# Three layers of a six-layer decoder: channel mix as a pipeline of single batches, relative attention's start reordered, mLSTM's mask and line products in 16-bit parts

## The chip, the cores and the metric

The kernel runs on one core of a Trainium2 chip. Its time is the device time in microseconds from the start of the program to its end. A core has a matrix engine (PE; its weight loads are shown as PEld), a vector engine (DVE), an activation engine (ACT), a general engine (POOL) and a queue that issues most DMAs (SP). They run side by side and are ordered by semaphores that the kernel sets and waits for by hand.

## The reference, cut

x is (8, 256, 256): 8 batches, 256 tokens, 256 features. Two blocks of three layers, each followed by a sum with its input and a normalisation; what matters here are the third, fourth and fifth layers.

```
# third layer, channel mix
x_prev = x shifted by one token, zero first
xr = mu_r*x + (1-mu_r)*x_prev ;  xk = mu_k*x + (1-mu_k)*x_prev
out = sigmoid(xr @ W_r.T) * (square(relu(xk @ W_k.T)) @ W_v.T)

# fourth, attention of 16 heads with relative embeddings
scores = q.k + q.rel_k[clip(distance)] ;  out = (P @ v + P @ rel_v[...]) @ W_out

# fifth, mLSTM with 4 heads; q from x, k and v from the context
cs = cumsum(log_sigmoid(fg)) ;  log_D[s,t] = cs[s] - cs_before[t] + ig[t], -inf for t > s
D = exp(log_D - max_t log_D) ;  C = (q.k/8) * D
h = C @ v / (max(|sum C|, exp(-max log_D)) + eps), normalised per head
```

## The kernel before

`program` calls six layers one after another: retention, cross attention, channel mix, relative attention, mLSTM and a last expert layer. Each has a block of five instruction streams and writes its result to memory; the next layer's first DMA goes out after the previous one's last store has landed. All matmuls here are fp32 except one group in the last layer. A product of fp32 shows as two records in the trace, one of 16 bits and a transposition as one.

**Channel mix** (`channel_mix_layer`, lines 1039 to 1157). A hardware loop (Fori) of four turns over pairs of batches. In a turn PE transposes both inputs (L88), ACT copies them with a shift by one token (`shifted`, L1092) and scales them by 1-mu (`before`, L1099), DVE adds mu times x (`mixed`, L1117), PE forms k (L95) and r (L103), ACT does Relu (L1104) and Sigmoid (L1106), DVE squares (`k_act`, L1125), PE forms v (L103), DVE does product, sum and statistics of `y` (L1130, L1132, L122 to L127), POOL the inverse root (L1083), DVE the normalisation (L132). Each engine does a stage for both batches before the next stage. x has two buffers, loaded again when `y` has used them; the loads of five constants come first in SP's queue, x behind them, and every engine waits for all of them.

**Relative attention** (`relative_attention_layer`). Units of four heads go through a pipeline with steps -5 to 38. Before it, SP loads two x batches, 22 arrays (embedding tables in slices of rows and 16-row copies among them) and four more x; POOL clears `qr`, `probs`, `bias` and `v` as a whole and, once all 22 are there, makes small tables (L1331 to L1340); PE forms four constant products (L1522), DVE `const_row` (L1434), and only then PE transposes the first x (L88), projects q, k and v (L95, L103) and forms the first table (L1569). A table is stored and read back skewed as `bias`; the first use of that is the sum at L1444.

**mLSTM** (`mlstm_layer`). A prologue transposes x, forms the gates of all batches (L1953, L1956) and from them, on 64 rows (32 lines twice), the running maximum m of a (L1882); columns of a and of the floor are transposed and copied (L2016, L1887). Then 16 units of two heads, two units per batch. For unit U, PE's `distances` (L1990, L1994) adds -m over the keys, as a product of a 32-row selector `minus` with m, and a mask of -1e30, as a product of the identity and `mask`; ACT takes its exponential (`decay`, L1845); `products` (L1979) is q.k; DVE multiplies (`c`, L1897); `outputs` (L2005 to L2007) is c times v in products of 65 columns. `products` has one buffer and waits for c of the unit before. At every second step DVE's norm chain (L1915 to L1934) normalises the heads of a batch, ACT squares (L1836), and two to six steps later come the variance (L1938), the scaling (L1903, then L1809 and L1812 on POOL), the statistics and the end (L132). The order of a step: PE distances(s+1), products(s), outputs(s-1); ACT Square of batch (s-2)/2, decay(s+1); DVE c(s), scale, end, norm, variance, statistics. SP loads x and the context in turns, then mask, `minus` (1 MB) and out_w, then v.

## Time and profile before

| | us |
|---|---|
| three timed runs | 2073.78, 2080.76, 2081.3; median 2080.76 |
| profiled execution | 2090.12 |
| its span, first to last instruction | 2088.3 |
| mean granted clock of PE in it | 0.895 |
| busy in it: PE, PEld, DVE, ACT, POOL | 1691.1, 1307.3, 1280.4, 684.5, 291.6 |

Busy time of an engine is the union of its instructions; a share near one doesn't say that the engine runs at its best, since PE's clock is granted at one of two levels, 1.0 (2.4 GHz) or 0.5 (1.2 GHz). Times in the rows are microseconds from the span's start, L numbers are lines of the kernel.

### The profile page before, as it was taken

How to read it: one execution, taken by the hardware profiler on the slowest of the kernel's cores; microseconds unless marked ns; L12 is line 12 of the kernel's file. 1: busy time of each engine (PE TensorE's matmuls, PEld its weight loads, DVE VectorE, ACT ScalarE, POOL GpSimd, SP SyncE). 2: the span in 40 equal slices, each digit the busy share in tenths (PEclk: the TensorE clock that was granted, in tenths of full speed). 3: DMA queues.
4: the chain of work that ended last, by engine and by line, in shares of the span. 5: the costliest groups of instructions: out<-in, count | busy, mean ns of one | idle time of the engine just before them, and what ended most of it. 6: DMA issues, size and time to landing. Idle time of an engine off the chain costs nothing. (4 is left out here: it accounts for less than half of the span.)

```text
span 2088.3 us, 34248 instructions
## 1 busy us (share of the span) xinstructions
PE 1691.1 (81%) x12550; PEld 1307.3 (63%) x12550; DVE 1280.4 (61%) x3839; ACT 684.5 (33%) x1444; POOL 291.6 (14%) x244
## 2 busy tenths in 40 slices
PE   5798987489984637888888769849799999999987
PEld 4676765356653525666666646648577777777766
DVE  3556544145533413555565525644899999999995
ACT  3323321145552314555555412102322222222210
POOL 1433433100000030000000002321010010010010
PEclk9999998689996677999999966569999999999999
DMA  3000000201001127988888660053000000000000
GB/s 110 6 11 22 6 6 11 77 17 32 13 12 57 40 68 263 331 294 296 293 298 309 217 158 6 21 192 133 1 1 11 1 11 11 1 11 11 1 6 11
DMA packets 97221, 176.17 MB, mean 84 GB/s; under 512 B 16484, under 2 KB 81508, under 8 KB 92260
## 3 DMA queue, kind: packets, MB, share of 16 engines
q1 hardware_dynamic: 97060, 174.02, 24.0%
q8 instruction: 101, 1.65, 0.3%
q14 instruction: 60, 0.49, 0.1%
HBM read 94.17 MB, written 79.69 MB: 83 GB/s over the span
## 5 line engine op out<-in xcount | busy, mean ns | idle before, releaser
L2511 PE MATMUL bank<-per_up,per_act_w 128*128 128x256 f32 x1024 | 246.7, 386 | 22.0 <-DVE per_yout L2402 11.9
L95 PE MATMUL bank<-per_xT,per_down 128*128 128x256 f32 x1024 | 256.2, 396 | 2.3 <-ACT per_xT L2209 1.6
L2511 PEld LDWEIGHTS bank<-per_up,per_act_w 128*128 128x128 f32 x1024 | 194.4, 192 | 52.8 <-DVE per_act_w L2392 27.1
L95 PEld LDWEIGHTS bank<-per_xT,per_down 128*128 128x128 f32 x1024 | 189.2, 194 | 25.6 <-issue 2.7
L2216 ACT ACTIVATE per_act_w<-bank 128x512 f32<-128x512 f32 x128 | 76.2, 597 | 352.0 <-PE bank L95 306.3
L2381 DVE TENSOR_TENSOR per_hot_x<-per_picksT,per_iota_x 128x4096 f16<-128x4096 f16 x64 | 155.8, 2434 | 0.0
L1444 DVE CUSTOM_DVE_ANT_0 rel_summed<-bank,rel_bias 128x256 f32<-128x256 f32 x256 | 93.1, 423 | 61.6 <-PE bank L1550 48.6
L1362 ACT ACTIVATE rel_probs<-rel_summed,rel_low 128x256 f32<-128x256 f32 x256 | 114.1, 519 | 10.6 <-DVE rel_low L1444 10.6
L95 PE MATMUL bank<-ret_x2T,ret_w_in 128*128 128x256 f32 x384 | 98.2, 416 | 15.3 <-DVE ret_x2T L437 15.3
L2498 PEld LDWEIGHTS bank<-per_hot_y,per_hot_x 128*128 128x128 f16 x2048 | 68.6, 96 | 62.5 <-issue 48.6
L870 DVE TENSOR_REDUCE xat_mx<-bank 128x2 f32<-128x512 f32 x128 | 79.5, 684 | 44.9 <-PE bank L914 44.8
L2498 PE MATMUL bank<-per_hot_y,per_hot_x 128*128 128x32 f16 x2048 | 71.2, 177 | 34.1 <-DVE per_act_w L2392 34.1
L95 PEld LDWEIGHTS bank<-ret_x2T,ret_w_in 128*128 128x128 f32 x384 | 78.8, 210 | 30.2 <-DVE ret_x2T L437 16.7
L2392 DVE TENSOR_TENSOR per_act_w<-bank,per_act_w 128x512 f32<-128x512 f32 x128 | 88.0, 691 | 12.3 <-PE bank L2498 2.0
L2195 POOL TENSOR_TENSOR per_sim<-per_sim,per_best_i 128x512 f32<-128x512 f32 x32 | 44.3, 1407 | 365.8 <-DVE per_sim L2331 365.8
L1582 PE MATMUL bank<-rel_ident,rel_probs 128*128 128x128 f32 x512 | 85.5, 315 | 0.8 <-DVE rel_pT L1453 0.5
L1582 PEld LDWEIGHTS bank<-rel_ident,rel_probs 128*128 128x128 f32 x512 | 71.8, 211 | 21.5 <-issue 21.1
L1370 ACT ACTIVATE rel_pT<-bank 128x512 f32<-128x512 f32 x64 | 38.2, 597 | 142.7 <-PE bank L1582 142.6
L1550 PE MATMUL bank<-rel_kT,rel_qT 32*128 32x256 f32 x512 | 55.5, 469 | 27.5 <-issue 9.8
L1594 PE MATMUL bank<-rel_ident,rel_by_dist 128*128 128x128 f32 x256 | 47.8, 311 | 33.7 <-DVE rel_wT L1512 33.7
L842 ACT ACTIVATE xat_probs<-bank 128x512 f32<-128x512 f32 x128 | 66.2, 612 | 12.5 <-PE bank L930 12.5
L1594 PEld LDWEIGHTS bank<-rel_ident,rel_by_dist 128*128 128x128 f32 x256 | 36.0, 208 | 45.3 <-issue 45.3
(350 smaller groups left out, 3287.4 us busy)
## 6 DMA issues: line engine op xcount, KB each, us to landing
rel_qr_rows<-rel_qr SPq DMA_DIRECT2D x32, 1024.0 KB, 6.8
rel_p_rows<-rel_probs SPq DMA_DIRECT2D x32, 1024.0 KB, 4.7
rel_bias<-rel_qr_rows SPq DMA_DIRECT2D x64, 384.0 KB, 4.2
rel_by_dist<-rel_p_rows SPq DMA_DIRECT2D x64, 384.0 KB, 4.8
per_down<-in_per_down SPq DMA_DIRECT2D x1, 4096.0 KB, 25.4
per_up<-in_per_up SPq DMA_DIRECT2D x1, 4096.0 KB, 13.5
ret_xin<-in_x SPq DMA_DIRECT2D x8, 256.0 KB, 2.8
x_after_ret<-ret_yout SPq DMA_DIRECT2D x8, 256.0 KB, 2.1
```

What stands on the lines that cost most here:

```text
L95: last = pe.matmul(dst, wt[:, c], src[:, c, :], start=c == 0, stop=c == DC - 1)
L842: nc.scalar.activation(probs[:, U % 2, r], tiles(second_bank(U, r)), ACT.Exp)\
L870: dve.tensor_reduce(mx[:, b % 2, :, 4 * (U % GROUPS) + r], tiles(first_bank(U, r)), AX.X, ALU.max).then_inc(max_taken, 1)
L1362: last = nc.scalar.activation(probs[:, U % 2, r // 2, at:at + SEQ, r % 2], summed[:, r, t], ACT.Exp, bias=low[:, r, t:t + 1], scale=-1.0)
L1444: last = dve.tensor_tensor_reduce(summed[:, r, t], tiles(bank[r])[:, t], bias[:, U % 2, t, r // 2, :, r % 2], 1.0, 3.0e38, ALU.add, ALU.mi ...
L1582: last = pe.transpose(bank[4 + r % 2][:, (2 * c + t) * P:(2 * c + t) * P + P], probs[:, U % 2, r // 2, at:at + P, r % 2], ident[:])
L1594: last = pe.transpose(bank[6][:, (2 * e + t) * P:(2 * e + t) * P + P], by_dist[:, U % 3, t, k, first:first + P, e], ident[:])
L2216: nc.scalar.activation(act_w[:, m % 2, 2 * k:2 * k + 2, :], tiles(bank[3 + k % 2]), ACT.Gelu_apprx_tanh).then_inc(gelu_ready, 1)
L2381: dve.tensor_tensor(hot_x[:, slot].rearrange("p s (c e) -> p s c e", e=4), four(0, wide_x), pattern(iota_x, wide_x), ALU.is_equal)
L2392: dve.tensor_tensor(g, bank[5 + k % 2][:].rearrange("p (s j) -> p j s", j=COLS), g, ALU.mult)\
L2498: last = pe.matmul(bank[5 + u % 2][:, s * COLS:s * COLS + COLS], hot_x[:, slot, at], hot_y[:, slot, at], start=True, stop=True)
L2511: last = pe.matmul(tiles(bank[7])[:, t, :], act_w[:, n % 2, k, t * P:t * P + P], up[:, k, :], start=k == 0, stop=k == COLS - 1)
```

## The change

Channel mix: the loop over pairs is unrolled into steps -2 to 8, with one batch per step and per stage, and x gets four buffers. SP issues x of batch 0, the identity, mu, x of batch 1, the three weights, then x of 2 and 3; engines wait for what they need. Relative attention: slices of tables are laid out on the host and loaded whole, 10 constant loads instead of 22, in order of need; POOL's clearing goes to DVE and is cut to the parts that nothing else writes; the constant products move behind the first table (bank 7 in place of bank 0). mLSTM: m is split into three bf16 parts that add up to it exactly, on 96 rows; selector, identity and mask become bf16, converted on ACT; the selector is made from a 96 x 32 diagonal in place of the 1 MB load. Values of the first unit wait for the constant row. A step's order becomes, on PE, products(s), distances(s+1), outputs(s-1), and on ACT decay(s+1), then Square.

```diff
@@ channel_mix_layer
+    XS = 4
-    loads = [(ident[:], ident_in), (mu[:], w["mu"]), (wr[:], w["wr"]), (wk[:], w["wk"]), (wv[:], w["wv"])]
+    STEPS = range(-2, nb + 1)
@@ sync
-            load_all(sp, loaded, loads)
-            stream_batches(sp, x_in, x_out, xin, yout, x_loaded, x_used, y_ready, stored, nb)
+            sp.dma_start(xin[:, 0], batch_of(x_in, 0)).then_inc(x_loaded[0], 16)
+            sp.dma_start(ident[:], ident_in).then_inc(ident_loaded, 16)
+            sp.dma_start(mu[:], w["mu"]).then_inc(mu_loaded, 16)
+            sp.dma_start(xin[:, 1], batch_of(x_in, 1)).then_inc(x_loaded[1], 16)
+            weights = load_all(sp, weights_loaded, [(wk[:], w["wk"]), (wr[:], w["wr"]), (wv[:], w["wv"])])
+            for b in range(2, XS):
+                sp.dma_start(xin[:, b], batch_of(x_in, b)).then_inc(x_loaded[b], 16)
+            for s in STEPS:
+                if (b := batch(s - 1)) is not None:
+                    if b + XS < nb:
+                        sp.wait_ge(x_used, b + 1)
+                        sp.dma_start(xin[:, b % XS], batch_of(x_in, b + XS)).then_inc(x_loaded[b % XS], 16)
+                    sp.wait_ge(y_ready, b + 1)
+                    sp.dma_start(batch_of(x_out, b), yout[:, b % 2]).then_inc(stored[b % 2], 16)
@@ scalar
+                if (b := batch(s)) is not None:
...
+                    nc.scalar.activation(relu_k[:, b % 2], tiles(k_bank(b)), ACT.Relu).then_inc(relu_ready, 1)
...
+                    nc.scalar.activation(r[:, b % 2], tiles(r_bank(b)), ACT.Sigmoid).then_inc(r_ready, 1)
+                if (b := batch(s + 2)) is not None:
...
+                    nc.scalar.activation(shifted[:, b % 2, :, 1:SEQ + 1], tiles(turn_bank(b)), ACT.Copy)\
+                        .then_inc(xT_ready, 1)
...
@@ vector
+            for s in STEPS:
+                if (b := batch(s - 1)) is not None:
+                    dve.wait_ge(r_ready, b + 1)
+                    dve.wait_ge(v_mm, b + 1)
...
+                    row_stats(dve, y[:, b % 2], st, mv[:, b % 2], ve[:, b % 2]).then_inc(var, 1)
+                if (b := batch(s)) is not None:
+                    dve.wait_ge(relu_ready, b + 1)
+                    if b >= 2:
+                        dve.wait_ge(v_mm, b - 1)
...
+                if (b := batch(s + 1)) is not None:
+                    dve.wait_ge(before_ready, b + 1)
+                    if b >= 2:
+                        dve.wait_ge(r_mm, b - 1)
...
+                if (b := batch(s - 1)) is not None:
+                    dve.wait_ge(rstd, b + 1)
...
@@ tensor
+            pe.wait_ge(ident_loaded, 16)
+            for s in STEPS:
+                if (b := batch(s)) is not None:
+                    if b == 0:
+                        pe.wait_ge(weights_loaded, 16 * 3)
+                    pe.wait_ge(mixed_ready, b + 1)
+                    if b >= 2:
+                        pe.wait_ge(k_act_ready, b - 1)
...
+                if (b := batch(s + 2)) is not None:
+                    pe.wait_ge(x_loaded[b % XS], 16 * (b // XS + 1))
+                    if b >= 2:
+                        pe.wait_ge(xT_ready, b - 1)
+                    turn(pe, tiles(turn_bank(b)), xin[:, b % XS], ident).then_inc(turned, 1)
+                if (b := batch(s)) is not None:
+                    pe.wait_ge(k_act_ready, b + 1)
+                    if b >= 2:
+                        pe.wait_ge(gated_ready, b - 1)
+                    by_token(pe, tiles(v_bank(b)), k_act[:, b % 2], wv).then_inc(v_mm, 1)
@@ relative_attention_layer
+    loads = [(cols[:], w["cols"]), (wq[:], w["wq"]), (wk[:], w["wk"]), (reach_k[:], w["reach_k"])]
+    late_loads = [(near_v[:], w["near_v"]), (base_v[:], w["base_v"].partition_broadcast(P)),
+                  (bo[:], w["bo"].partition_broadcast(P)), (wo[:], w["wo"])]
@@ sync
+            sp.dma_start(xin[:, 0], batch_of(x_in, 0)).then_inc(x_loaded[0], 16)
+            sp.dma_start(ident[:], ident_in).then_inc(ident_loaded, 16)
             load_all(sp, loaded, loads)
-            for b in range(2, XS):
+            sp.dma_start(wv[:], w["wv"]).then_inc(wv_loaded, 16)
+            load_all(sp, late, late_loads)
+            for b in range(1, XS):
@@ gpsimd
-            pool.memset(qr[:], 0.0)
-            pool.memset(probs[:], 0.0)
-            pool.memset(bias[:], 0.0)
-            pool.memset(v[:], 1.0)
@@ vector
-            dve.tensor_tensor(const_row[:], tiles(bank[0]), bo[:].unsqueeze(1).broadcast_to([P, TT, D]), ALU.add)\
-                .then_inc(const_ready, 1)
+            dve.memset(qr[:, :, :, BAND:BAND + P], 0.0)
+            dve.memset(qr[:, :, :, 2 * BAND + P:ROW], 0.0)
+            dve.memset(v[:, :, :, :, HD:VW], 1.0)
+            dve.memset(bias[:, :, 0, :, NEAR:SEQ], 0.0)
+            dve.memset(bias[:, :, 1, :, 0:REACH], 0.0)
+            dve.memset(probs[:, :, :, SEQ:WIDE - SEQ], 0.0)
...
+                if table_of(s) == 0:
+                    dve.wait_ge(late, 16 * len(late_loads))
+                    dve.wait_ge(const_mm, 1)
+                    dve.tensor_tensor(const_row[:], tiles(bank[7]), bo[:].unsqueeze(1).broadcast_to([P, TT, D]),
+                                      ALU.add).then_inc(const_ready, 1)
@@ tensor
                 if (U := table_of(s)) is not None:
                     table(U, s)
+                    if U == 0:
+                        constants()
@@ mlstm_layer
+    PARTS = 3 * R
+    exact_loads = [(mask[:], w["mask"]), (diag[:], w["diag"])]
@@ sync
+                if b == nb // 2:
+                    load_all(sp, exact_loaded, exact_loads)
@@ scalar
+            act.wait_ge(exact_loaded, 16 * len(exact_loads))
+            nc.scalar.activation(ident16[:], ident[:], ACT.Copy)
+            nc.scalar.activation(mask16[:], mask[:], ACT.Copy)
+            nc.scalar.activation(minus[:], over(diag[:], P), ACT.Copy, scale=-1.0).then_inc(exact_ready, 1)
@@ vector
-            dve.tensor_copy(m[:, SEQ:SPAN], m[:, P:SEQ]).then_inc(m_ready, 1)
+            middle, low_part = slice(R, LINES), slice(LINES, PARTS)
+            dve.tensor_copy(m_parts[0:LINES, 0:SEQ], m[:])
+            dve.drain()
+            dve.tensor_tensor(m_rest[:], m[:], m_parts[0:LINES, 0:SEQ], ALU.subtract)
+            dve.drain()
+            dve.tensor_copy(m_parts[middle, 0:SEQ], m_rest[middle])
+            dve.drain()
+            dve.tensor_tensor(m_parts[low_part, 0:SEQ], m_rest[middle], m_parts[middle, 0:SEQ], ALU.subtract)
+            dve.drain()
+            dve.tensor_copy(m_parts[:, SEQ:SPAN], m_parts[:, P:SEQ]).then_inc(m_ready, 1)
@@ tensor
                 for k in range(HP):
-                    copy = slice(R * k, R * k + R)
-                    pe.matmul(d_bank(U, k)[:, 0:SPAN], minus[copy, NH * b + HP * pair + k], m[copy],
+                    pe.matmul(d_bank(U, k)[:, 0:SPAN], minus[:, NH * b + HP * pair + k], m_parts[:],
                               start=True, stop=False)
-                for k in range(HP):
                     behind = d_bank(U, k)[:].rearrange("p (t s) -> p t s", t=TT)[:, :, 0:P]
-                    last = pe.matmul(behind, ident[:], mask[:], start=False, stop=True)
+                    last = pe.matmul(behind, ident16[:], mask16[:], start=False, stop=True)
...
             for s in STEPS:
+                if (U := unit(s)) is not None and U >= 1:
+                    products(U)
                 if (U := unit(s + 1)) is not None:
                     distances(U)
-                if (U := unit(s)) is not None and U >= 1:
-                    products(U)
                 if (U := unit(s - 1)) is not None:
                     outputs(U)
```

## Rows read from the trace of the kernel before

**Rows 1.** Windows by layer: stretch, length, busy PE PEld DVE ACT POOL, clock, DMA

```profile
642.30:748.26 105.96, 61.21 (x224) 49.19 (x224) 44.55 (x112) 37.35 (x64) 7.40 (x11) 0.69 0.14 48
748.26:1214.70 466.44, 357.56 (x3208) 276.39 (x3208) 241.55 (x841) 227.74 (x513) 33.79 (x29) 0.89 0.75 265
1214.70:1384.90 170.20, 126.65 (x548) 90.62 (x548) 86.49 (x221) 32.07 (x82) 42.98 (x38) 0.64 0.22 58
1384.90:2088.30 703.40, 631.37 (x4538) 515.96 (x4538) 604.91 (x1945) 160.36 (x254) 56.48 (x48) 0.97 0.08 29
```

**Rows 2.** Mix: window of a pair; timeline: start, us, line [idle before]

```profile
676.43:700.10 23.67, 15.35 (x56) 12.26 (x56) 11.17 (x29) 9.37 (x17) 1.55 (x2) 0.72 0.13 44
...
676.43 3.27 DVE L1117 SCALAR_TENSOR_TENSOR mix_mixed<-mix_shifted,mix_mu,mix_before 128x256 f32<-128x256 f32 x8 [3.08 <-ACT mix_before L1099]
...
678.16 3.78 PE L95 MATMUL bank<-mix_mixed,mix_wk 128*128 128x256 f32 x8 [3.98 <-DVE mix_mixed L1117]
...
687.66 3.62 PE L103 MATMUL bank<-mix_wv,mix_k_act 128*128 128x256 f32 x16
...
689.66 0.69 DVE L1130 TENSOR_TENSOR mix_y<-bank,mix_r 128x512 f32<-128x512 f32 x1 [2.20 <-PE bank L103]
...
692.46 0.69 DVE L1130 TENSOR_TENSOR mix_y<-bank,mix_r 128x512 f32<-128x512 f32 x1
```

**Rows 3.** Timeline of mix: its first POOL product, the last batch's y

```profile
647.95 0.19 POOL L1079 TENSOR_SCALAR mix_mu_rest<-mix_mu 128x4 f32<-128x4 f32 x1 [4.65 <-DMA mix_wv<-in_mix_wv]
...
740.13 0.69 DVE L1130 TENSOR_TENSOR mix_y<-bank,mix_r 128x512 f32<-128x512 f32 x1
```

**Rows 4.** Timeline of relative attention's start

```profile
748.30 3.51 POOL L1325 MEMSET rel_qr<- 128x4096 f32 x1
...
763.86 0.22 POOL L1331 TENSOR_SCALAR rel_minus_own<-rel_own 128x2 f32<-128x2 f32 x1 [1.60 <-DMA rel_base_v<-in_rel_ext_v]
...
774.36 1.99 PE L95 MATMUL bank<-rel_xT,rel_wq 128*128 128x256 f32 x8 [0.77 <-ACT rel_xT L1378]
...
780.68 0.93 PE L1569 MATMUL bank<-rel_band_k,rel_qT 32*128 32x191 f32 x16 [0.88 <-DVE rel_v L1466]
...
793.67 0.43 DVE L1444 CUSTOM_DVE_ANT_0 rel_summed<-bank,rel_bias 128x256 f32<-128x256 f32 x1 [9.11 <-DMA rel_bias<-rel_qr_rows]
```

**Rows 5.** Timeline of mLSTM's prologue

```profile
1234.59 0.60 ACT L1821 ACTIVATE mls_xT<-bank 128x512 f32<-128x512 f32 x1 [3.73 <-PE bank L88]
...
1240.30 0.47 ACT L1825 ACTIVATE mls_size<-bank,mls_b_gate 64x256 f32<-64x256 f32 x1 [5.11 <-PE bank L1956]
...
1246.10 0.21 DVE L1885 COPY mls_m<-mls_m 64x128 f32<-64x128 f32 x1
...
1247.85 1.65 PE L1990 MATMUL bank<-mls_m,mls_minus 32*128 32x384 f32 x4 [0.48 <-DVE mls_percol L1887]
```

**Rows 6.** Timeline of mLSTM, one unit on PE and a wait of DVE

```profile
1281.32 1.65 PE L1979 MATMUL bank<-mls_xT,mls_cT 64*128 64x256 f32 x8
...
1284.39 1.02 DVE L1897 SCALAR_TENSOR_TENSOR mls_c<-bank,mls_decay 128x384 f32<-128x384 f32 x2 [1.94 <-ACT mls_decay L1845]
...
1285.65 1.65 PE L1990 MATMUL bank<-mls_m,mls_minus 32*128 32x384 f32 x4
...
1289.24 1.23 PE L1979 MATMUL bank<-mls_xT,mls_cT 64*128 64x256 f32 x4
```

**Rows 7.** Timeline of mLSTM's tail on DVE

```profile
1365.04 0.69 DVE L1903 TENSOR_TENSOR mls_hn<-mls_hn,mls_s 128x512 f32<-128x512 f32 x1 [0.54 <-POOL mls_s L1804]
...
1367.31 0.22 DVE L1915 SCALAR_TENSOR_TENSOR mls_norm<-bank,mls_percol 128x4 f32<-128x4 f32 x2
...
1374.96 0.69 DVE L1903 TENSOR_TENSOR mls_hn<-mls_hn,mls_s 128x512 f32<-128x512 f32 x1 [0.54 <-POOL mls_s L1804]
```

**Rows 8.** The page's costliest groups, the 16-bit matmuls: busy, mean ns | idle before

```profile
L2498 PE MATMUL bank<-per_hot_y,per_hot_x 128*128 128x32 f16 x2048 | 71.2, 177 | 34.1 <-DVE per_act_w L2392 34.1
```

**Rows 9.** Window in mLSTM, columns as in rows 1

```profile
1297.64:1321.53 23.89, 22.27 (x79) 14.92 (x79) 13.26 (x35) 6.24 (x18) 7.25 (x6) 0.50 0.04 12
```

More of the change, by code:

```diff
@@ L1073, in _ @@
+            sp.wait_ge(weights_loaded, weights)
+            for u in range(2):
+                sp.wait_ge(stored[u], 16 * (nb // 2))
         @block.gpsimd
         def _(pool):
+            pool.memset(shifted[:, :, :, 0:1], 0.0)
             pool.memset(half[:], -0.5)
-            pool.memset(shifted[:], 0.0)
             pool.drain()
-            pool.wait_ge(loaded, 16 * len(loads))
+            pool.wait_ge(mu_loaded, 16)
             pool.tensor_scalar(mu_rest[:], mu[:], -1.0, 1.0, ALU.mult, ALU.add).then_inc(consts, 1)
-            with pool.Fori(0, nb // 2) as i:
-                for u in range(2):
-                    pool.wait_ge(var, 2 * i + u + 1)
-                    pool.tensor_tensor(rs[:, u], ve[:, u], half[:], ALU.pow).then_inc(rstd, 1)
+            for b in range(nb):
+                pool.wait_ge(var, b + 1)
+                pool.tensor_tensor(rs[:, b % 2], ve[:, b % 2], half[:], ALU.pow).then_inc(rstd, 1)
@@ L1093, in _ @@
                         .then_inc(xT_ready, 1)
-                for u in range(2):
-                    act.wait_ge(xT_ready, 2 * i + u + 1)
+                    act.wait_ge(xT_ready, b + 1)
                     for k in range(2):
                         for c in range(DC):
-                            last = nc.scalar.activation(before[:, u, k, c, :], shifted[:, u, c, 0:SEQ], ACT.Copy,
-                                                        scale=mu_rest[:, 2 * k + c:2 * k + c + 1])
+                            last = nc.scalar.activation(before[:, b % 2, k, c, :], shifted[:, b % 2, c, 0:SEQ],
+                                                        ACT.Copy, scale=mu_rest[:, 2 * k + c:2 * k + c + 1])
@@ L1149, in _ @@
                     for g in range(DC):
-                        last = project(pe, tiles(bank[4 * u + 2])[:, g], wk[:, :, g * P:g * P + P], mixed[:, u, 1])
+                        last = project(pe, tiles(k_bank(b))[:, g], wk[:, :, g * P:g * P + P], mixed[:, b % 2, 1])
                     last.then_inc(k_mm, 1)
-                    by_token(pe, tiles(bank[4 * u + 1]), mixed[:, u, 0], wr).then_inc(r_mm, 1)
-                for u in range(2):
-                    pe.wait_ge(k_act_ready, 2 * i + u + 1)
-                    by_token(pe, tiles(bank[4 * u + 3]), k_act[:, u], wv).then_inc(v_mm, 1)
+                    if b >= 2:
+                        pe.wait_ge(r_ready, b - 1)
@@ L1599, in values @@
                 b, g = U // GROUPS, U % GROUPS
+                if U == 0:
+                    pe.wait_ge(const_ready, 1)
                 pe.wait_ge(v_ready, b + 1)
@@ L1687, in sem @@
         return nc.alloc_semaphore("mls_" + name)
-    ident, mask, minus = sb("ident", [P]), sb("mask", [TT, P]), sb("minus", [R, P], rows=LINES)
+    ident, mask, diag = sb("ident", [P]), sb("mask", [TT, P]), sb("diag", [R], rows=PARTS)
+    ident16, mask16, minus = sb("ident16", [P], BF16), sb("mask16", [TT, P], BF16), sb("minus", [R, P], BF16, PARTS)
+    m_parts, m_rest = sb("m_parts", [SPAN], BF16, PARTS), sb("m_rest", [SEQ], rows=LINES)
     w_gate = sb("w_gate", [3, DC, 2, NH])
```

184 lines of the change are left out of this document (92 added, 92 removed).

## The prediction

> **What bounds the kernel now.** I read the windows by layer first [rows 1]: six layers run one after another and share nothing, so each layer is its own sum. The change touches mix (106.0 us), relative attention (466.4 us) and mLSTM (170.2 us); the last layer (703.4 us) is left alone, as are the first two. In mix PE is busy 61 of 106 us, DVE 45, ACT 37: nobody is full, so a chain bounds it, at a granted clock of 0.69. In relative attention the long steady part isn't touched; only its first 32 us are. In mLSTM PE is busy 127 of 170 us at 0.64.
>
> Then the timeline of each. **Mix** [rows 2]: two batches go through all stages together and the next two start only when their inputs come in. From mixed products to the next pair's is 23.7 us, 11.8 per batch, and in it DVE works 11.17, ACT 9.37, PE 15.35. Matmuls of one weight take 3.78 us at the lower level of the clock (1.2 GHz), right after idle, and 3.62 for two sets at the upper one (2.4 GHz). **Relative attention** [rows 4]: the layer starts at 748.26 [rows 1]; POOL waits until 763.86 for the last of 22 loads, then POOL, PE and DVE do constants before the first transposition, so that the first projection starts at 774.36 and the first table at 780.68. **mLSTM** [rows 6]: a unit (two per batch) at the lower clock is products and outputs 4.33 us (1281.32 to 1285.65) and distances 3.59 (to 1289.24): 7.92 us. In 1297.64 to 1321.53 PE is busy 22.27 of 23.89 us and the clock is at 0.50 [rows 9]: PE's queue is full, and at half speed. Every second unit has another stall besides: DVE waits 1.94 us for the exponentials [rows 6], which ACT does after a Square that waits for DVE's own norm chain. The norm chain of the last batch starts at 1367.31 [rows 7].
>
> **The change, part by part.**
>
> *Mix, steady state.* The pair loop becomes a pipeline of one batch per step: k and r of b, transposition of b+2, v of b, while DVE finishes b-1 and mixes b+1. No operation is added; the table loads on ACT, two per pair, should become fewer, but ACT (9.37/2 = 4.7 us per batch with them) is no bound. DVE: 11.17/2 = 5.6 us plus some five drains, 6.0. PE at the upper clock: 3.62/2 = 1.81 for each of three sets, of which some 0.1 is the tail of the last, so 3 x 1.72 and 0.5 for the transposition: 5.7. The closed chain: v of b-1 ends, DVE's y block takes 2.80 (689.66 to 692.46), k_act 0.7 (as the product of that size), v of b 1.9, hops 0.2: 5.6, but PE must fit k, r and the transposition between, 1.72+1.72+0.5+1.9+0.2 = 6.0. Three figures near 6; I take **6.2**, bounds 5.9 and 6.8. The four x buffers give a load over 9 us between x_used and its turn. New waits (gated_ready, k_act_ready, mixed_ready of b-2) look two batches back and should be over.
>
> *Mix, start.* Before, x came behind the weights; POOL sees them landed at 647.95 [rows 3], 5.6 us after the layer's start. Now x, identity and mu are first; the first matmuls then wait for weights, behind one or two x loads, about 649, and for the mix of batch 0 (transposition, copy, four scalings, four products: some 5 us after x lands at about 645.4): 650.6. k and r run partly at the lower clock: 3.8+2.3; then 0.5 and v 1.9, so y(0) at 659.1. y(7) starts at 659.1 + 7 x 6.2 = 702.5 instead of 740.13 [rows 3]; behind it both kernels do the same. **Gain 37.6, bounds 33 and 40.**
>
> *Relative attention, start.* 22 loads become 10, ordered by need. The transposition needs x and the identity; ACT's copy needs cols, wq, wk, reach_k (about 0.97 MB; mix's first 0.83 MB took 5.6 us [rows 3]) and two small POOL products: 6.6 us after start. Projection at 7.3 instead of 26.1. Before, the constants' matmuls had raised the clock; now q, k and v meet it low: 774.36 to 780.68 is 6.3 us, at half clock for most of it 9 to 10. Table at 17.2 instead of 32.4 [rows 4]. DVE's six memsets (4624 elements a row) lie in the wait for the loads; without cover they would cost some 4 us, at the rate of POOL's row (4096 in 3.51). The constants move behind the first table: PE waits there with table 1 and scores 0 behind it, DVE with its second table copy; both have the time until the first skewed load has come (first table to first sum, 13.0 us [rows 4]), and the constants need some 5. POOL's add of const_row waits too, and is needed only units later. SP issues fewer descriptors and no queue is moved past another. **Gain 15.2, bounds 11 and 18.**
>
> *mLSTM, distances.* Per unit two fp32 products on 32 rows (side by side) and two mask products become two 16-bit products on 96 rows (384 columns) and two on 128 (256). No row shows a wide 16-bit matmul. Floor: the 16-bit one with 32 columns and its weight load take 71.2/2048 = 35 ns [rows 8]: four are 0.14 us, 0.3 at half clock. Ceiling: a column as dear as in an fp32 record (0.83 ns at the upper clock, two records per matmul become one), 1280 columns, 2.1 us at the lower clock. At the ceiling's rate 32 columns alone would be 27 of those 35 ns, leaving 8 for a 128-column weight load; half the rate is likelier: 1.07, and with starts **1.2** instead of 3.59.
>
> The Trainium skill (FP8 and Floating Point Precision, BF16 Matmul, with TensorE Precision Notes) says true fp32 takes four passes, bf16 one. By it the distances would be an estimated 1280 columns in one pass, 1.07 us at 1.2 GHz; the sum would stay within 2 us of mine. No run here shows it yet.
>
> *mLSTM, steady state.* PE per unit at the lower clock: 4.33+1.2 = 5.53, 11.1 per batch. DVE per batch: 1365.04 to 1374.96 is 9.92 [rows 7], less a wait of 0.54 and one for Square, an estimated 0.7, 8.7, plus two c of 1.02 and a hop: 10.8. Putting Square behind the exponentials and products ahead of distances takes the 1.94 us stall away: decay of a unit is then ready before DVE asks. What ends last is PE at the lower clock (11.1), DVE at the upper one (10.8). Period **11.1**, bounds 10.8 and 12.9 (ceiling).
>
> *mLSTM, both ends.* The first distances started at 1247.85 and normalisation 7 at 1367.31: 119.5 us. Now: distances 1.2, exponentials 1.4, c 1.0, hops: products(1) at 3.8; then units of 5.5 on PE, outputs(1) end at 14.9. Six periods of 11.1, and a last one of 10 (no distances left): 91.5. The split of m on DVE, five operations and four drains, costs 2.15 us in place of the 0.21 copy [rows 5]; 1.0 of it is covered, since distances start 1.5 us after that copy, waiting for the columns. So 0.9 later. ACT's three conversions (128 + 256 + 4096 elements a row; 512 take 0.60, so at most 8 x 0.60 + 0.7, at least 3.6) lie in the 5.11 us that ACT idled before L1825 [rows 5]; bounds 0 and 0.4. The 1 MB minus load goes. **Gain 119.5 - 91.5 - 0.9 = 27, bounds 16 and 36** (PE at the upper clock from the start saves 7 more and makes DVE the bound).
>
> **Sum.** 37.6 + 15.2 + 27 = 80. The profiled execution took 2090.12 us (span 2088.3), so 2010 in its terms. It lies 9.4 above the median 2080.76 of the three timed runs, which spread 2073.78 to 2081.3; I forecast the median: 2080.8 - 80 = **2001**.
>
> **Rivals.** *(a) mLSTM's distances stay dear*: 16-bit columns at the ceiling, or weight loads that nothing hides. PE per unit 6.4, 12.9 per batch; gain 27 - 7 x 1.8 = 14 there, and the time 2014. For: nothing in the trace shows a wide 16-bit product. Against: the 35 ns row. *(b) mLSTM does better*: dense products and distances raise the clock, PE stays ahead, 10.6 per batch, first normalisation 5 earlier; 35 there, 1992. For: the clock does go to 1 at times in this layer (0.64 mean). *(c) mix is bound by a low clock*: PE per batch at 1.2 GHz is 3 x 3.4 + 0.9 = 11.1; then it gains 4 instead of 38, 2035. For: 0.69 now. Against: its idle comes from the chain that goes, and PE would be 92% busy. The Trainium skill (TensorE: Matmul & The Clock Gate, HAM oscillation) says idle between bursts brings the clock down; that rule speaks for (c) only if the new chain leaves gaps. *(d) slower than before*: the last layer holds its clock at 0.97 over 703 us [rows 1]; all gains are lost once 160 us more of it run at half speed (80 us at a doubled PE time). A shifted start would have to turn its short idles into drops. Nothing in its rows changes, so I give it 1 in 100: 2090. *(e) The pipeline isn't one*: a wait in mix's new order closes a loop one batch long and steps take 9 to 10 us; gain 12, 2027.
>
> **How the numbers follow.** Forecast 0.5 (own range 1993 to 2009), (a) 0.14, (b) 0.2, (c) 0.04, (e) 0.06, (d) 0.01, other sizes 0.05. The range takes (a) and (b) and leaves (c), (d), (e) out: 1985 to 2020. About 0.5%, 10 us, can be told from no change: faster 0.98, same 0.01, slower 0.01.
>
> **What would show it.** Mix: y blocks (the DVE product of v and r) 6.2 us apart and layer length near 68 us at a clock above 0.9. Relative attention: first table 17 us after layer start, first sum at 30. mLSTM: distances 1.2 us at the low clock, norm chains 11.1 apart, no 1.94 us wait of c for decay; first distances 1 us later in the layer. Wrong if mix's steps are over 7 us, if c still waits for the exponentials, if the norm chains are 13 apart, or if the last layer's span moves by over 5 us.

## The result, and the profile after

The changed kernel takes 1988.2 us (median of four runs, 1985.5 to 1995.0), the kernel before 2079.8 (2073.8 to 2081.3): 91.6 us less, ratio 0.957 with a 95% interval of 0.954 to 0.960. The forecast was 2001 with a range of 1985 to 2020; the time lies in it, 13 us below the forecast. (The median before is now of four runs; the forecast started from 2080.8, that of the first three.) The profiled execution took 1995.0 us (span 1993.2, mean granted clock 0.907); before it was 2090.1 (2088.3, 0.895).

Windows by layer of the changed kernel, columns as in rows 1 (stretch, length, busy PE PEld DVE ACT POOL, granted clock, DMA share, GB/s); the first line is the first two layers together, then mix, relative attention, mLSTM and the last layer:

```profile
0.00:643.80 643.80, 515.03 (x4032) 375.29 (x4032) 302.94 (x720) 226.95 (x531) 150.94 (x118) 0.91 0.08 27
643.80:708.50 64.70, 49.94 (x224) 41.95 (x224) 43.19 (x112) 28.53 (x57) 5.96 (x13) 0.87 0.24 79
708.50:1157.70 449.20, 357.37 (x3208) 275.64 (x3208) 245.97 (x847) 227.57 (x513) 19.97 (x26) 0.90 0.78 275
1157.70:1291.90 134.20, 97.98 (x484) 80.69 (x484) 85.68 (x225) 36.74 (x85) 43.01 (x38) 0.61 0.23 66
1291.90:1993.20 701.30, 630.02 (x4538) 515.43 (x4538) 604.92 (x1945) 160.37 (x254) 56.48 (x48) 0.97 0.08 29
```

Beside [rows 1]:

| layer | before | after | gain | forecast gain |
|---|---|---|---|---|
| first two | 642.3 | 643.8 | -1.5 | 0 |
| mix | 105.96 | 64.70 | 41.3 | 37.6 |
| relative attention | 466.44 | 449.20 | 17.2 | 15.2 |
| mLSTM | 170.20 | 134.20 | 36.0 | 27 |
| last | 703.40 | 701.30 | 2.1 | 0 |
| span | 2088.3 | 1993.2 | 95.1 | 80 |

Nearly all of the gain (94.5 of 95.1 us) sits in the three changed layers, and each has more than was forecast. PE's busy time in mLSTM fell from 126.65 to 97.98 us, while its clock did not rise (0.64 to 0.61); in mix the clock went from 0.69 to 0.87.

**Mix.** The timeline of one step of the changed kernel (start, us, line; PE, then DVE's product of v and r in three successive steps with one of its `k_act` between), and the window of that step:

```profile
671.95 1.89 PE L95 MATMUL bank<-mix_mixed,mix_wk 128*128 128x256 f32 x8
...
673.67 1.89 PE L103 MATMUL bank<-mix_wr,mix_mixed 128*128 128x256 f32 x8
...
675.40 0.60 PE L88 MATMUL bank<-mix_ident,mix_xin 128*128 128x128 f32 x4
...
675.84 1.95 PE L103 MATMUL bank<-mix_wv,mix_k_act 128*128 128x256 f32 x8
```

```profile
660.89 0.69 DVE L1151 TENSOR_TENSOR mix_y<-bank,mix_r 128x512 f32<-128x512 f32 x1 [1.87 <-PE bank L103]
...
672.22 0.69 DVE L1151 TENSOR_TENSOR mix_y<-bank,mix_r 128x512 f32<-128x512 f32 x1
...
675.05 0.69 DVE L1160 SCALAR_TENSOR_TENSOR mix_k_act<-bank,mix_relu_k 128x512 f32<-128x512 f32 x1
...
677.90 0.69 DVE L1151 TENSOR_TENSOR mix_y<-bank,mix_r 128x512 f32<-128x512 f32 x1
```

```profile
672.00:677.68 5.68, 5.68 (x30) 4.98 (x29) 5.35 (x15) 3.40 (x8) 0.70 (x1) 1.00 0.29 95
```

k takes 1.72 us from its start to r's, r 1.73, the transposition 0.44, and v of this batch until k of the next (677.63) 1.79: 5.68, with PE busy for all of it at the upper clock. DVE is as full: 5.35 us busy, and the other 0.33 are four gaps of 0.08 to 0.09 us behind its drains (a drain lets it finish one instruction before the next starts). Where the kernel before needed 23.67 us for two batches [rows 2], this takes 11.36.

**Relative attention's start** (the layer begins at 708.50):

```profile
711.49 1.12 PE L88 MATMUL bank<-rel_ident,rel_xin 128*128 128x128 f32 x4 [10.98 <-DMA rel_ident<-in_ident]
...
714.54 0.22 POOL L1374 TENSOR_SCALAR rel_minus_own<-rel_cols 128x2 f32<-128x2 f32 x1 [5.89 <-DMA rel_reach_k<-in_rel_reach_k]
...
715.84 3.54 PE L95 MATMUL bank<-rel_xT,rel_wq 128*128 128x256 f32 x8 [3.24 <-ACT rel_xT L1423]
...
723.72 0.93 PE L1627 MATMUL bank<-rel_band_k,rel_qT 32*128 32x191 f32 x16 [0.88 <-DVE rel_v L1514]
...
726.68 0.69 DVE L1566 TENSOR_TENSOR rel_const_row<-bank,rel_bo 128x512 f32<-128x512 f32 x1 [0.94 <-PE bank L1578]
...
735.25 0.42 DVE L1492 CUSTOM_DVE_ANT_0 rel_summed<-bank,rel_bias 128x256 f32<-128x256 f32 x1 [6.70 <-DMA rel_bias<-rel_qr_rows]
```

POOL still waits for a load, but for the first group of them, 6.0 us into the layer and not 15.6 [rows 4]; the first table comes at +15.2 instead of +32.4, the first sum at +26.8 instead of +45.4, still released by the skewed load.

**mLSTM.** The timeline of PE over one unit, from its products to the next unit's; the start of the norm chain in that unit on DVE; and the window of one batch, from one norm chain's sum over hn to the next (1225.28 to 1235.64):

```profile
1238.49 1.65 PE L2065 MATMUL bank<-mls_xT,mls_cT 64*128 64x256 f32 x8
1240.08 0.50 PE L2075 MATMUL bank<-mls_m_parts,mls_minus 96*128 96x384 bf16 x1
1240.37 0.42 PE L2078 MATMUL bank<-mls_mask,mls_ident 128*128 128x256 bf16 x1
1240.59 0.53 PE L2075 MATMUL bank<-mls_m_parts,mls_minus 96*128 96x384 bf16 x1
1240.91 0.42 PE L2078 MATMUL bank<-mls_mask,mls_ident 128*128 128x256 bf16 x1
1241.12 0.53 PE L2089 MATMUL bank<-mls_v,mls_c 128*128 128x65 f32 x2
...
1243.71 1.65 PE L2065 MATMUL bank<-mls_xT,mls_cT 64*128 64x256 f32 x8
```

```profile
1243.82 0.23 DVE L2001 SCALAR_TENSOR_TENSOR mls_norm<-bank,mls_percol 128x4 f32<-128x4 f32 x2 [0.31 <-PE bank L2091]
```

```profile
1225.28:1235.64 10.36, 10.36 (x49) 8.56 (x48) 9.36 (x26) 3.23 (x9) 4.94 (x4) 0.50 0.08 27
```

The four 16-bit products take 1.04 us (1240.08 to 1241.12) where the fp32 ones took 3.59 [rows 6]; one column costs 0.83 ns at the lower clock (256 columns in 0.21, 384 in 0.32). The unit is 5.22 us long, not 7.92, so a batch is 10.44 us of PE. Below, a gap is the time from one norm chain to the next, taken at DVE's sum over hn (L2016), the heads' outputs being normalised. The gaps are 8.52, 10.36, 10.36, 10.49, 10.36, 10.36 and 10.05 us, against 14.7 and 15.9 in turn before. c no longer waits for the exponentials.

### The profile page after: what moved, and what is told of

Read it like the earlier page. It is cut to its first block and busy times, and to the rows that moved or that the text cites. A ratio compares the mean times of both kernels' runs of the same rounds, so it can differ in the third digit from the quotient of the medians.

```text
span 1993.2 us, 34055 instructions
## 1 busy us (share of the span) xinstructions
PE 1650.3 (83%) x12486; PEld 1289.0 (65%) x12486; DVE 1282.7 (64%) x3849; ACT 680.2 (34%) x1440; POOL 276.3 (14%) x240
## 5 line engine op out<-in xcount | busy, mean ns | idle before, releaser
L1492 DVE CUSTOM_DVE_ANT_0 rel_summed<-bank,rel_bias 128x256 f32<-128x256 f32 x256 | 93.0, 421 | 58.6 <-PE bank L1606 45.4
L95 PE MATMUL bank<-ret_x2T,ret_w_in 128*128 128x256 f32 x384 | 98.0, 415 | 15.3 <-DVE ret_x2T L437 15.3
L2582 PE MATMUL bank<-per_hot_y,per_hot_x 128*128 128x32 f16 x2048 | 71.2, 177 | 33.8 <-DVE per_act_w L2476 33.7
L842 ACT ACTIVATE xat_probs<-bank 128x512 f32<-128x512 f32 x128 | 66.2, 612 | 12.5 <-PE bank L930 12.5
L408 DVE TENSOR_TENSOR ret_probs<-bank,ret_seen 128x256 f32<-128x256 f32 x128 | 45.2, 414 | 32.9 <-PE bank L513 32.8
```

What stands on the lines that cost most here:

```text
L95: last = pe.matmul(dst, wt[:, c], src[:, c, :], start=c == 0, stop=c == DC - 1)
L842: nc.scalar.activation(probs[:, U % 2, r], tiles(second_bank(U, r)), ACT.Exp)\
L1492: last = dve.tensor_tensor_reduce(summed[:, r, t], tiles(bank[r])[:, t], bias[:, U % 2, t, r // 2, :, r % 2], 1.0, 3.0e38, ALU.add, ALU.mi ...
L2582: last = pe.matmul(bank[5 + u % 2][:, s * COLS:s * COLS + COLS], hot_x[:, slot, at], hot_y[:, slot, at], start=True, stop=True)
```

## The experiments

Each kernel is the changed one with the edit shown; ratios are to the kernel before. Layer lengths and gaps come from one profiled execution each; the gaps of mLSTM mostly repeat to 0.05 us within a run (the one of 10.49 above does not), the length of the layer less well: in five kernels with mLSTM as changed (`after`, which is the changed kernel, and the four of the third group) it took 131.6, 134.2, 134.4, 136.7 and 137.4 us. The first gap alone was 8.5 us where the clock stood near 1.00 and 10.5 where it stood at 0.50. So the gaps carry the readings on mLSTM.

### The 16-bit products and the order, each alone

m32_new_order: the mLSTM functions and arrays of the kernel before, with only these two moves:

```
@@ scalar (mLSTM)
+                (exponentials of unit s+1)
                 (Square of norm_of(s))
-                (exponentials of unit s+1)
@@ tensor (mLSTM)
+                if (U := unit(s)) is not None and U >= 1:
+                    products(U)
                 if (U := unit(s + 1)) is not None:
                     distances(U)
-                if (U := unit(s)) is not None and U >= 1:
-                    products(U)
```

> The changed kernel with mLSTM's line and mask products in fp32 again (the 1 MB selector too), in the new order of a step. Theory: at the lower clock PE's queue is the bound, 7.9 us per unit, so the new order alone brings little: norm chains about 15 us apart, the layer 25 to 33 us longer than the 134.2 us of the changed kernel, the kernel about 2017 us. Rival: the wait of c for the exponentials behind Square (1.94 us per batch) was the real cost: then the order alone keeps about half of the 36 us, norm chains about 13 apart, about 2006 us.

Measured: 2015.2 us (ratio 0.968, 0.962 to 0.975); mLSTM 163.2 us, gaps 9.9, 10.7, then four of 15.24. A window of about one such gap:

```profile
1231.00:1246.20 15.20, 15.20 (x57) 11.30 (x58) 9.12 (x25) 3.34 (x9) 4.90 (x4) 0.50 0.05 17
```

PE is busy all through, at 0.50: two units of 7.6. The order alone takes c's stall on the exponentials away and gains 7.0 us in the layer, most of it in the first two gaps; then PE is late next, and DVE's norm chain waits 2.75 us for it.

m16_old_order: 16-bit products, both moves undone.

```
@@ scalar (mLSTM)
-                (exponentials of unit s+1)
                 (Square of norm_of(s))
+                (exponentials of unit s+1)
@@ tensor (mLSTM)
-                    products(U)
-                    distances(U)
+                    distances(U)
+                    products(U)
```

> The changed kernel with the 16-bit products, but both PE and ACT in the old order of a step. Theory: with short distances DVE is the bound (about 10.2 us of work per batch), so a stall of 1.94 us per batch behind Square adds to it: norm chains about 12.1 apart, the kernel 12 us above the changed one, about 2000 us. Rival: the order is worth nothing once distances are short: within 3 us of the changed kernel.

Measured: 2003.4 us (0.963, 0.957 to 0.968); layer 150.0, gaps 12.2 to 12.4.

m16_act_old: only ACT's move undone (Square ahead of the exponentials). m16_pe_old: only PE's (distances ahead of products).

> The changed kernel with only ACT in the old order (Square ahead of the exponentials), PE in the new one. Theory: the stall is ACT's alone, so this costs as much as both old orders, about 12 us. Rival: it costs nothing without PE's old order.

> The changed kernel with only PE in the old order (distances ahead of products), ACT in the new one. Theory: c waits for products at most the length of the distances, 1.05 us, in steps where DVE is ahead, 0 to 5 us in all. Rival: PE's order is what counts, 10 us or more.

Measured: ACT's alone undone 2002.2 us (0.962, 0.956 to 0.967), layer 147.1, gaps 12.38; PE's alone 1996.7 us (0.959, 0.954 to 0.965), layer 142.8, gaps 11.30. The last is more than the 0 to 5 us expected: 8.5 us in the time and 8.6 in the layer. In the timeline of DVE with ACT's old order the stall of [rows 6] is back, to the hundredth:

```profile
1234.32 1.02 DVE L1983 SCALAR_TENSOR_TENSOR mls_c<-bank,mls_decay 128x384 f32<-128x384 f32 x2 [1.94 <-ACT mls_decay L1922]
```

and with PE's old order c waits for products that are queued behind distances:

```profile
1222.95 1.02 DVE L1983 SCALAR_TENSOR_TENSOR mls_c<-bank,mls_decay 128x384 f32<-128x384 f32 x2 [0.91 <-PE bank L2065]
```

What follows: on top of the 16-bit products ACT's move is worth 12.38 - 10.36 = 2.02 us a batch and PE's 0.94, and with ACT's old order PE's is worth nothing (12.38 either way). With fp32 products both together are worth nothing in the steady part, 15.24 against a mean of 15.3; but the clock was 0.50 in those gaps and 0.53 to 0.68 before, so the slower clock may hide a part of what the order gave. Per batch the 16-bit products alone give 2.9 us and both together 4.9, 2.0 more than the two alone. In the layer's length it is 7.0 us for the order, 20.2 for the products and 36.0 for both, 8.8 more, each from one profile and with the scatter of some 6 us above. Each removes a different limit, PE's queue and DVE's wait, and while one stands the other's removal is partly hidden.

### What sets the 10.36 us

Above, PE at the lower clock is busy 10.36 of 10.36 us, which looked like the bound. Four kernels change PE's load or DVE's.

mls_no_mask (the mask product of each distance left out, so the masked scores are not those of the reference):

```
-                    behind = ...
-                    last = pe.matmul(behind, ident16[:], mask16[:], start=False, stop=True)
```

> The changed kernel, but in the mLSTM layer the mask product of each of the four distances is left out, so two 16-bit products a unit remain of four; the masked half of the scores is then wrong. Two theories of what sets the 10.36 us between two norms of the changed kernel. PE sets it: its unit at the lower clock is 1.58 (products) + 1.05 (distances) + 2.58 us (outputs), of which about 0.45 goes, so the norm chains stand 9.5 us apart, or, where DVE then becomes the bound, about 10.1. DVE sets it: they stay 10.36 apart. By both the other layers keep their lengths within their scatter (440 to 450 us for relative attention).

mls_fill (each mask product five times):

```
-                    last = pe.matmul(behind, ident16[:], mask16[:], start=False, stop=True)
+                    for more in range(5):
+                        last = pe.matmul(behind, ident16[:], mask16[:], start=False, stop=more == 5 - 1)
```

> The changed kernel, but in the mLSTM layer each mask product stands five times in a row (the sum of the mask stays large and negative, so the output is the same); 8 more 16-bit products a unit, 16 a batch, of 0.10 to 0.15 us at the lower clock each. What is asked is whether more work in PE's queue lifts the clock of this layer. If it does, PE's steady unit falls below DVE's work and the norm chains stand about 10.1 us apart, layer 132 to 134 us. If the clock stays at 0.5, they stand 10.36 + 2.4 to 3.4, so 12.8 to 13.8 us apart, and the layer takes 152 to 160 us.

mls_end_act (the last normalisation on ACT):

```
@@ gpsimd
+                    (shift = -rs * mean, two small products behind rs)
@@ scalar, behind Square
+                    for t in range(TT):
+                        last = nc.scalar.activation(yout[:, b % 2, t], y[:, b % 2, t], ACT.Identity,
+                                                    bias=shift[:, b % 2, t:t + 1], scale=rs[:, b % 2, t:t + 1])
@@ vector
-                    normalise(dve, yout[:, b % 2], y[:, b % 2], mv[:, b % 2], rs[:, b % 2])[-1]...
```

> The changed kernel, but the last normalisation of mLSTM's output goes from DVE to ACT (two Identity activations with scale and bias a batch; POOL makes the shift), which takes about 1.7 us a batch from DVE's 10.1. If PE at the lower clock sets the 10.36 us, the norm chains stay 10.3 to 10.4 apart and only the tail of the layer changes, by under 1 us, time 1986 to 1989. If DVE sets it, they come to 8.5 to 9 us apart, the layer to about 123 us and the time to about 1977.

mls_end_act_fill is both of the last two.

> The normalisation on ACT and each mask product five times. If the filling lifts PE's clock, PE's unit is about 2.6 + 16-bit products of 0.05 us (0.4) + 0.3, so some 3.5 to 4 us, DVE (8.4 us a batch) is the bound, and the norm chains stand about 8.5 apart, the layer takes about 122 us and the kernel about 1976. If the clock stays at 0.5 they stand 12.8 to 13.8 apart, and the kernel takes 2005 to 2012.

Measured, by the gap between norm chains, with the mean granted clock inside it:

| kernel | gaps at clock 1.00 | gaps at 0.50 | layer | time |
|---|---|---|---|---|
| after | - | 10.36, three times; 10.49 once | 134.2 | 1988.2 |
| mls_no_mask | - | 10.35 to 10.37 | 135.7 | 1995.9 (one run) |
| mls_fill | 10.36, 10.36, 10.35 | - | 133.7 | 1988.3 (one run) |
| mls_end_act | 9.14 | 10.55, 10.55 | 129.7 | 1987.4 |
| mls_end_act_fill | 9.17, 9.14 | - | 132.5 | 1985.3 |

(The first gap of each, the last, with no distances left, and those in which the clock moved are left out.) Windows between two norm chains, of mls_fill, of mls_no_mask, and of mls_end_act at either clock:

```profile
1240.36:1250.71 10.35, 7.64 (x64) 6.38 (x64) 9.58 (x26) 3.23 (x9) 4.94 (x4) 1.00 0.08 25
```

```profile
1234.37:1244.73 10.36, 9.92 (x44) 8.06 (x44) 9.60 (x26) 3.23 (x9) 4.94 (x4) 0.50 0.08 26
```

```profile
1217.92:1227.06 9.14, 5.97 (x48) 4.83 (x48) 8.38 (x23) 4.10 (x11) 5.31 (x7) 1.00 0.09 30
1237.62:1248.17 10.55, 10.55 (x49) 8.56 (x48) 7.96 (x23) 4.21 (x11) 5.33 (x6) 0.50 0.08 27
```

With PE at the upper clock and idle for a quarter of the time, the gap is the same 10.35; with 0.86 us a batch less for PE to do at the lower clock it is the same 10.36. So DVE needs 10.36 us by itself: its instructions and the drains between them fill it.

At the lower clock PE needs 0.08 us more, 10.44. In `after` the norm chains' first instruction (L2001) starts 10.46, 10.44, 10.44 and 10.44 us after the one before in the steady part, each time when a wait of 0.23 to 0.34 us for PE ends; the sum over hn still comes mostly 10.36 apart, since a small instruction between the two gets shorter as DVE gets later (last section). rel_before (next group) has the same mLSTM layer; its third gap, at 0.50, is 10.44, with a wait for PE in front of the norm chain, and its fifth and sixth, at 0.66, are 10.36 with none. The window of that third gap, and the start of the chain behind it:

```profile
1239.83:1250.27 10.44, 10.44 (x50) 8.61 (x49) 9.29 (x26) 3.23 (x9) 4.95 (x4) 0.50 0.08 27
```

```profile
1248.13 0.23 DVE L1985 SCALAR_TENSOR_TENSOR mls_norm<-bank,mls_percol 128x4 f32<-128x4 f32 x2 [0.35 <-PE bank L2075]
```

So PE ends last at the lower clock and DVE at the upper one, but they are level within 0.1 us, and relieving PE alone gains 0.08 a batch at most. Taking the normalisation off DVE shows the same from the other side: 9.14 where the clock is up, and 10.55 with PE busy 10.55 of 10.55 where it is down. The expectations missed sizes: I had put DVE's work at 10.1, so looked for a change to 10.1 that never came, and for 8.5 with the normalisation gone, where 9.14 came (why, is in the last section). That the filling lifts the clock is not shown: the mean over the middle gaps was 0.90 with it and 0.52 without, but mix_before (next group), with mLSTM as in the changed kernel, had 0.73 over the same gaps, mls_end_act without any filling had 1.00 in one gap and 0.81 in another, and mls_end_act_fill dipped to 0.84 in three of its gaps; each is one profile. In either case the gap does not get shorter. The last two kernels (1987.4, ratio 0.956 with 0.950 to 0.961; 1985.3, 0.954 with 0.949 to 0.960) can't be told from the changed one.

### Mix and relative attention

mix_before and rel_before: the changed kernel with that one layer of the kernel before (for relative attention, its arrays too). rel_const_first: the new loads stay, the constants go ahead of the first transposition:

```
@@ tensor (relative attention)
+            constants()
+            pe.wait_ge(const_ready, 1)
             for s in STEPS:
...
                     table(U, s)
-                    if U == 0:
-                        constants()
```

with DVE's const_row moved ahead of its loop likewise. mix_xs3: `XS = 3` for `XS = 4` in mix.

> The changed kernel with the channel-mix layer of the kernel before alone. If the gain of each part stands by itself, channel mix takes about 106 us for 64.7, with a table load in each turn and back in the lower clock, and the whole takes 1988 + 41 = 2029 us. If part of the 41 us was only a shift of waiting (next layer started late or in another state of the clock), the whole takes less than 2020.

> The changed kernel with the relative attention layer of the kernel before alone. If the start alone is what the new one gains, the first sum comes at +45 us for +26.8, the rest of the layer keeps its length, and the whole takes 1988 + 18 = 2006 us (2000 to 2012). If the start's wait was cover for something later in the layer (batches whose loads or clock came late anyway), the whole takes under 1998.

> The changed kernel, but the relative attention layer makes its constants (4 PE products and DVE's const_row) before its first transposition, as the kernel before did, while the new loads stay (one array for each table, q and k ahead of v, output weights and the rest last). If the constants' place carries the gain of this start, the first table waits for the late loads and comes about 7 us later than +15.3 us, and the layer takes 447 to 457 us where the changed kernel has 440 to 450. If the merged loads alone carry it, the first table stays at +15 to +17 and the layer's length doesn't move. The other layers don't differ.

> The changed kernel with three x buffers in channel mix for four. An x buffer comes free when the batch's output is written, and its load takes some 2.8 us. If PE's queue sets the 5.68 us between two outputs, three buffers cost nothing or under 0.2 us a step; if the fourth buffer carries the distance of the loads, a step takes 6.2 to 6.7 us and the layer 5 to 8 us more.

| kernel | its layer | time | ratio, 95% |
|---|---|---|---|
| mix_before | mix 106.2 | 2033.3 | 0.977, 0.973 to 0.980 |
| rel_before | relative attention 462.5 | 2004.4 | 0.963, 0.960 to 0.967 |
| rel_const_first | relative attention 454.9 | 2007.0 | 0.965, 0.962 to 0.969 |
| mix_xs3 | mix 69.8 | 1997.6 (one run) | - |

Mix stands by itself: undoing it costs 41.5 us in its layer and 45 of time, the layer being that of [rows 1] again. Relative attention undone costs 16 us of time, of 18 expected. The start falls into two parts, by the first sum: +43.6 with everything old, +38.9 with only the loads new, +26.8 with both. So at the first sum the merged and reordered loads, with the clearing moved to DVE, give 4.7 us and the place of the constants 12.1. I had expected 7 for it. In time only the constants' place is shown: put back alone it costs 18.8 us (2007.0), and the whole old layer 16.2 (2004.4); the two can't be told apart, so what the loads give is seen at the start of the layer in one profile each and not in the time. How the 4.7 divide between fewer loads, their order and the clearing no run tells. The trace of rel_const_first shows the rest: the late loads and POOL's const_in now stand ahead, and the constants run at the lower clock (3.75 us for 1.99), and only behind them comes the transposition:

```profile
721.52 0.25 POOL L1383 TENSOR_TENSOR rel_band_v<-rel_near_v,rel_base_v 128x32 f32<-128x32 f32 x1 [2.01 <-DMA rel_wo<-in_rel_wo]
...
723.73 3.75 PE L1577 MATMUL bank<-rel_wo,rel_const_in 128*128 128x256 f32 x8 [20.14 <-POOL rel_const_in L1385]
...
728.34 1.11 PE L88 MATMUL bank<-rel_ident,rel_xin 128*128 128x128 f32 x4 [0.86 <-DVE rel_const_row L1486]
...
739.26 0.93 PE L1626 MATMUL bank<-rel_band_k,rel_qT 32*128 32x191 f32 x16 [0.88 <-DVE rel_v L1518]
```

That layer starts at 711.5, so the first table is at +27.8, 12.5 later than after's +15.2. Behind the first sum, nothing of the layer was changed, yet that part took 414.5 to 422.4 us in the kernels with the new layer: the scatter that, with 18.6 us gained at the first sum, made this gain 17.2 in one profile and up to 25 in others (440.9 us at the shortest).

With three x buffers in mix, the timeline of PE shows the wait that the fourth one avoids, in each of five steps:

```profile
669.54 0.66 PE L88 MATMUL bank<-mix_ident,mix_xin 128*128 128x128 f32 x4 [0.95 <-DMA mix_xin<-x_after_xat]
```

The step becomes 6.67 to 6.79 us, a little over the 6.2 to 6.7 expected, and the layer 5.1 longer. The fourth buffer is needed.

## Why the prediction came out as it did

**Mix, steady state: mechanism right, size too long.** Forecast 6.2 (5.9 to 6.8), measured 5.68. Of the figures that it rested on, two were right: the sum for PE, 3 x 1.72 + 0.5 = 5.7, and the chain from v through y and k_act to the next v, 5.6, which the trace has as 2.83 + 0.69 + 0.10 + 1.95 + 0.11 = 5.68. What was too long is the 6.0 of that chain with PE's work in it: it added v's full 1.9 us and hops, though k of the next batch follows v without waiting for its end. DVE was put at 6.0, and its instructions with the gaps behind the drains are 5.68; and 6.2 lay above all three. PE, DVE and the chain all close at 5.68, PE's own matmuls at 5.62 (the first of v starts 0.10 behind k_act and holds the next up by 0.06); which of them sets the step no run tells. Seven steps at 0.52 are 3.6 of the 3.7 us missing. The start was +16.8 forecast, +17.1 measured; the lower clock lay over the first k and was gone at 657.6. Table loads on ACT fell from eight to one; ACT is now busy 3.40 us of a step, and what the loads would have cost was not run.

**Relative attention: right, 2 us short.** The projection starts at +7.3 as forecast. Then q, k and v took 7.9 us, not the 9 to 10, since the clock rose 3.2 us after their start: table at +15.2 for +17.2. From the table to the first sum 11.5, not 13.0. The constants behind the first table cost nothing visible: DVE's const_row is done 7.9 us before the load lands that the first sum waits for. rel_const_first bears out that this cover is the larger part of the gain.

**mLSTM: the mechanism right, the period 0.7 too long, the gain 9 too small.** Distances 1.04 us for 1.2; the choice of half the fp32 rate per column, between a floor of 0.3 and a ceiling of 2.1, was the measured one. The estimate from the Trainium skill (FP8 and Floating Point Precision, TensorE Precision Notes: true fp32 in four passes), 1.07 with bf16 taken as one pass, agrees with the trace's 1.04. PE's unit is 5.22 for 5.53, so its batch 10.44 for 11.1; DVE's batch is 10.36 for 10.8. What ends last at the lower clock is PE, as forecast, though only 0.08 us behind DVE. From first distances to the start of the last norm chain: 84.3 us for 91.5. Of the 7.2, by the chains' first instructions, 3.3 are the first distance between two of them (7.85 for 11.1, at a high clock: mostly luck, since in mix_before and rel_before the clock was at 0.50 there and it took 10.44), 3.0 the next five (10.44 to 10.67), 0.4 the last and 0.5 what lies ahead of the first chain. The split of m was to come 0.9 later; the first distances came at +32.3 for +33.2 before. It is in the trace as said (1187.66 to 1189.54 on DVE), but this time scatters between +32.3 and +33.8 in all runs with it, more than the term.

**Rivals.** (b), 1992 us, gave the nearest number: period 10.6, gain 35. That is luck, since its mechanism isn't what happened: it wanted the clock up so that PE stays ahead and the first normalisation 5 us earlier, and the clock was 0.50 through the steady part and the first chain 0.5 earlier. PE was short enough at half speed. (a) fell with 1.04 us. (c) fell: the steps of mix ran at 1.00; the rule of the Trainium skill (TensorE: Matmul & The Clock Gate, HAM oscillation) had spoken for it only if the chain left gaps, and it leaves none. (e) fell with 5.68. (d): the last layer took 701.3, and 700.3 to 703.5 in all runs.

**The sum.** 80 forecast, 95.1 in the profiles, 91.6 in the medians; 3.7 from mix, 2.0 from relative attention, 9.0 from mLSTM, 0.6 from layers that weren't changed. The mechanism held in each part, and each gain was forecast too small, so the errors add up where they might have cancelled.

## What to carry to other kernels

When two limits lie close, remove both before judging either: here the new order gave nothing per batch in the steady part and the cheap products 2.9 us, but together 4.9. A full engine isn't shown to be the bound by being full; lighten it and see if the gap moves (PE was busy 10.36 of 10.36 us, and 0.86 us less of its work moved the gap by under 0.1, since DVE was as full). A few constants ahead of a pipeline's first load-to-use chain cost their whole time and the late loads they need (12.1 us at the first sum here); behind it they cost nothing that the trace shows.

## What the runs showed of the hardware

**TensorE's clock stayed at 0.50 while PE had no idle time for 48 us.** In the changed kernel it is 0.50 from 1217.4 to 1302.7, and from 1217.60 to 1266.25 PE is busy all through. The same mLSTM layer in mix_before was at a mean of 0.83 in a gap with PE idle for a third of it:

```profile
1217.60:1266.25 48.65, 48.64 (x224) 39.87 (x224) 43.67 (x119) 15.21 (x44) 24.74 (x20) 0.50 0.08 28
```

```profile
1257.05:1267.40 10.35, 7.01 (x51) 5.67 (x49) 9.59 (x25) 3.23 (x9) 4.94 (x4) 0.83 0.08 25
```

Rival (b) had counted on dense work to bring it up. The Trainium skill (TensorE: Matmul & The Clock Gate, Part 1: The HAM clock gate) names 2.4 GHz the busy state; the first window does not agree with it.

**A tiny DVE instruction waits for POOL.** The addition of 1e-8 to 8 values a row takes 0.17 us where POOL is idle, 0.34 to 0.54 in the steady part of after, 0.76 or 0.77 in four of the eight batches of mls_fill and up to 1.15 in mls_end_act. Timelines of after (no POOL work beside it; steady part), of mls_fill, and of mls_end_act:

```profile
1205.03 0.17 DVE L2008 TENSOR_SCALAR mls_norm<-mls_norm 128x8 f32<-128x8 f32 x1
...
1243.51 1.27 POOL L1885 TENSOR_TENSOR mls_y<-mls_y,mls_xin 128x512 f32<-128x512 f32 x1
...
1244.43 0.37 DVE L2008 TENSOR_SCALAR mls_norm<-mls_norm 128x8 f32<-128x8 f32 x1
```

```profile
1248.22 1.26 POOL L1885 TENSOR_TENSOR mls_y<-mls_y,mls_xin 128x512 f32<-128x512 f32 x1
...
1248.75 0.76 DVE L2008 TENSOR_SCALAR mls_norm<-mls_norm 128x8 f32<-128x8 f32 x1
```

```profile
1224.57 1.26 POOL L1883 TENSOR_TENSOR mls_y<-mls_hn,mls_scale 128x512 f32<-128x512 f32 x1
...
1224.72 1.15 DVE L2017 TENSOR_SCALAR mls_norm<-mls_norm 128x8 f32<-128x8 f32 x1
```

It ends each time 0.02 to 0.04 us behind POOL's product (1244.80 after 1244.78, 1249.51 after 1249.48, 1225.87 after 1225.83). This is the Trainium skill's rule (SBUF — State Buffer, Who interferes with whom) that `tensor_scalar` in a two-port mode and a GpSimd instruction lock each other out, and that the second to issue waits for the whole of the first; the trace agrees. It explains why the sums over hn stay 10.36 apart while PE's pace is 10.44: in after DVE waits 0.31 us for PE, and the instruction then takes 0.37 instead of 0.76.

The larger wait of this kind is in the normalisation (L132), two `tensor_scalar` instructions. In seven of eight batches of after the second takes 1.36 us instead of 0.41 and ends 0.15 behind POOL's product, which started just before it; in the last batch, with no POOL work beside them, the pair takes 0.73 in place of 1.68:

```profile
1241.83 1.68 DVE L132 TENSOR_SCALAR mls_yout<-mls_y,mls_mv,mls_rs 128x256 f32<-128x256 f32 x2
...
1241.99 1.37 POOL L1882 TENSOR_TENSOR mls_y<-mls_hn,mls_scale 128x512 f32<-128x512 f32 x1 [0.49 <-DVE mls_hn L1989]
...
1287.77 0.73 DVE L132 TENSOR_SCALAR mls_yout<-mls_y,mls_mv,mls_rs 128x256 f32<-128x256 f32 x2 [0.82 <-POOL mls_rs L1888]
```

With it the 9.14 of mls_end_act adds up: 10.36, less the 1.60 from the normalisation's start to the next instruction's, plus 0.39 (1.15 - 0.76) of longer wait behind it, is 9.15. Where DVE alone sets the gap, as in mls_fill, an estimated 0.95 + 0.59 (0.76 - 0.17) = 1.5 us a batch would be there for a placement of POOL's two products that meets neither; at the lower clock PE's 10.44 would hide it. That was not run.
